# Queries and keys of layer 0 for two pairs at once, 512 columns to a matmul, in a two-layer graph attention kernel

## What is computed

```
q, k, v = x @ Wq + bq, x @ Wk + bk, x @ Wv + bv          # 8 heads of 32
attn = softmax(where(adj == 0, -inf, q k^T / sqrt(32)))
x1 = layernorm(attn v @ Wo + bo + x) * gamma + beta
q, k, v = x1 @ Wq1.T + bq1, ...                          # layer 1
pros = softmax(where(adj == 0, -16384, q k^T))
z = v;  4 times: z = 0.9 * pros z + 0.1 * v
out = layernorm(x1 + z) * gamma1 + beta1
```

## Time and profile before

| | us |
|---|---|
| median of three runs | 782.94 |
| lowest, highest | 782.71, 784.09 |
| span of the profiled execution | 784.0 |
| PE busy in it | 754.1 |
| ACT, DVE, POOL busy | 665.7, 637.1, 547.8 |

### The profile page before, as it was taken

The page is one execution under the profiler, slowest core; times in us unless marked ns, Lnnn a source line. Parts: engine busy times, 40 slices in busy tenths (PEclk is TensorE's granted clock), DMA queues, the critical chain, the costliest instruction groups (busy, mean ns, idle before and its releaser), DMA issues.

```text
span 784.0 us, 32528 instructions
## 1 busy us (share of the span) xinstructions
PE 754.1 (96%) x11544; PEld 710.6 (91%) x11544; DVE 637.1 (81%) x3093; ACT 665.7 (85%) x2570; POOL 547.8 (70%) x417
## 2 busy tenths in 40 slices
PE   6889999999999999999999999999999999999974
PEld 6778999999999999999999999999999999998863
DVE  5778888888888888888888888888888888887765
ACT  4779998889889988988998898998889899899661
POOL 0336858666777777777787777787777778768774
PEclk9899999999999999999999999999999999999997
DMA  7101011010111101111111011111001111100002
GB/s 239 48 21 50 23 35 37 22 30 23 50 50 49 50 29 26 47 50 49 50 49 30 23 51 50 49 49 50 29 23 50 50 50 36 30 16 17 29 15 68
DMA packets 33245, 34.12 MB, mean 44 GB/s; under 512 B 2368, under 2 KB 28864, under 8 KB 33088
## 3 DMA queue, kind: packets, MB, share of 16 engines
q1 hardware_dynamic: 33088, 32.06, 13.8%
HBM read 23.67 MB, written 8.39 MB: 41 GB/s over the span
## 4 chain that ended last, share of the span: by engine, by line
PE 89%; DVE 3%; ACT 2%; issue 2%; DMA 1%; SPq 1%; POOL 1%; POOLq 0%; DVEq 0%; ACTq 0%
PE psF L342 23%; PE psF L411 18%; PE psF L351 16%; PE psF L401 15%; PE psS L391 9%; PE psF L456 7%; PE psF L436 2%; ACT ex L1011 2%; DMA w_raw<-in_w 1%; DVE sm L1400 1%; DMA out<-o_t 1%; SPq L284 0%; DVE o_t L1491 0%; DVE bst L1450 0%; POOL o_t L1927 0%
## 5 line engine op out<-in xcount | busy, mean ns | idle before, releaser
L1011 ACT ACTIVATE ex<-sm,nmax 128x128 f32<-128x128 f32 x1024 | 397.9, 397 | 3.3 <-DVE nmax L1400 2.3
L1859 POOL TENSOR_TENSOR pr<-ex,rec 128x1024 f32<-128x1024 f32 x128 | 245.3, 1918 | 101.1 <-DVE rec L1409 101.1
L1400 DVE CUSTOM_DVE_ANT_0 sm<-psS,mask 128x128 f32<-128x128 f32 x1024 | 228.3, 284 | 41.6 <-PE psS L391 41.4
L1011 ACT ACTIVATION_READ_ACCUMULATOR ex<-sm,nmax 128x1 f32 x1024 | 200.7, 196 | 0.0
L1022 ACT ACTIVATE pT<-psF 128x512 f32<-128x512 f32 x256 | 138.8, 596 | 34.5 <-PE psF L401 34.4
L401 PE MATMUL psF<-ident,pr 128*128 128x128 f32 x1024 | 137.8, 276 | 0.8 <-ACT pT L1022 0.5
L401 PEld LDWEIGHTS psF<-ident,pr 128*128 128x128 f32 x1024 | 112.7, 141 | 9.3 <-ACT pT L1022 0.9
L342 PE MATMUL psF<-xh,w_hi 128*128 128x256 f32 x512 | 112.6, 302 | 7.7 <-DVE w_lo L1339 5.7
L411 PE MATMUL psF<-pT,z 128*32 128x128 f32 x3072 | 103.1, 276 | 2.3 <-DVE z L1512 2.0
L342 PE MATMUL psF<-xh,w_lo 128*128 128x256 f32 x512 | 104.1, 285 | 0.0
L342 PE MATMUL psF<-xl,w_hi 128*128 128x256 f32 x512 | 103.6, 284 | 0.0
(11 more groups left out here) (76 smaller groups left out, 1425.7 us busy)
## 6 DMA issues: line engine op xcount, KB each, us to landing
xt_in<-in_x_t SPq DMA_DIRECT2D x32, 256.0 KB, 3.0
x_in<-in_x SPq DMA_DIRECT2D x32, 256.0 KB, 3.0
out<-o_t SPq DMA_DIRECT2D x30, 256.0 KB, 2.2
adj_in<-in_adj SPq DMA_DIRECT2D x32, 128.0 KB, 2.4
pT<-in_w SPq DMA_DIRECT2D x4, 256.0 KB, 4.0
row<-in_rows SPq DMA_DIRECT2D x1, 768.0 KB, 6.8
w_raw<-in_w SPq DMA_DIRECT2D x3, 256.0 KB, 7.0
out<-o_t SPq DMA_DIRECT2D x4, 128.0 KB, 1.7
```

The costliest lines, as they stand in the source:

```text
L1011: e = nc.scalar.activation(ex[l][:, b, h, :], sm[l][:, b, h, :], ACT.Exp, scale=-1.0, bias=nmax[l][:, b, h:h + 1], accum_out=tot[l][:, b, ...
L1400: last = nc.vector.tensor_tensor_reduce(sm[l][:, b, h, :], psS[:, o:o + N], mask[p.parity][:, b, :], -1.0, BIG, ALU.add, ALU.min, nmax[l][ ...
L1859: nc.gpsimd.tensor_tensor(pr[l][:, b, :, :], ex[l][:, b, :, :], rec[l][:, b, :].unsqueeze(2).broadcast_to([128, H, N]), ALU.mult).then_inc ...
```

## The change

Queries and keys of layer 0 are no longer made for one pair in each turn. An even turn t makes the queries of pairs t and t + 1, an odd turn the keys of pairs t - 1 and t, with 512 moving columns: `two_pairs(c, t)`, six matmuls for one half c of the output features, c = 0 into bank F[0], c = 1 into F[2]. For this xh and xl of layer 0 get two buffers of two pairs each, qT two of two pairs, kT one; x is rounded three pairs further ahead (`split_hi(t + 2)`, `split_lo(t + 3)`), and SP loads `xt_in` three pairs further ahead. Pairs 0 to 5 keep the old way; the first new group, the queries of pairs 6 and 7, stands in `begin()`, and `end()` loses the queries and keys of pair 31.

```diff
@@ SP
             def step(t):
-                load_xt(t + 2)
+                if t.number <= 3:
+                    load_xt(t + 2)
+                elif t.number <= 6:
+                    load_xt(t + (t.number - 2))
+                    load_xt(t + (t.number - 1))
+                else:
+                    load_xt(t + 5)
                 store(t - 9)
@@ PE
+            def two_pairs(c, p):
+                if p.real:
+                    first = p - p.parity
+                    x_ready(0, first + 1)
+                    i = p.number // 2 % 2
+                    for n, (a, e) in enumerate(parts):
+                        for kc in range(C):
+                            last = nc.tensor.matmul(ps_two[c][:, :], (w_hi, w_lo)[e][:, p.parity, kc, c * 128:(c + 1) * 128],
+                                                    (xh0, xl0)[a][i][:, kc, :], start=(n == 0 and kc == 0),
+                                                    stop=(n == 2 and kc == C - 1))
+                    last.then_inc((qr, kr)[c][0].sem, 2)
...
             def scores(l, p):
                 if p.real:
-                    pe.wait_ge(q_s[l].sem, q_s[l].at(p))
-                    pe.wait_ge(k_s[l].sem, k_s[l].at(p))
+                    saved = p + (1 - p.parity) if l == 0 and p.number >= FIRST_TWO else p
+                    pe.wait_ge(q_s[l].sem, q_s[l].at(saved))
+                    pe.wait_ge(k_s[l].sem, k_s[l].at(saved))
@@ PE, begin
                 free((q_s[0], Pair(5)))
+                two_pairs(0, Pair(6))
+                free((q_s[0], Pair(6)))
                 hop(0, Pair(1))
...
                 free((k_s[0], Pair(5)))
+                two_pairs(1, Pair(6))
+                keys(1, 1, Pair(3))
+                free((k_s[0], Pair(6)))
                 turn_hop(0, Pair(1))
-                keys(1, 1, Pair(3))
@@ PE, step
-                queries(0, 0, t - 1)
+                two_pairs(0, t)
                 free((hT_s[3], t - 7))
                 values(1, 0, t - 4)
-                queries(0, 1, t - 1)
                 values(1, 1, t - 4)
...
-                keys(0, 0, t - 1)
-                keys(0, 1, t - 1)
+                two_pairs(1, t)
@@ PE, end
                 values(1, 1, Pair(28))
-                free((z_s[1], Pair(26)))
-                queries(0, 0, Pair(31))
-                queries(0, 1, Pair(31))
                 free((y_s, Pair(29)))
                 turn_probs(1, 1, 0, Pair(27))
                 free((pT_s[1][0][1], Pair(27)))
                 turn_probs(1, 1, 1, Pair(27))
-                free((v_s[1], Pair(28)))
-                keys(0, 0, Pair(31))
-                free((q_s[0], Pair(31)))
+                free((z_s[1], Pair(26)))
                 turn_probs(1, 0, 0, Pair(27))
-                keys(0, 1, Pair(31))
                 free((pT_s[1][1][1], Pair(27)))
                 turn_hop(3, Pair(25))
@@ ACT
             def split_hi(p):
                 if p.real:
                     act.wait_ge(xt_s.sem(p), xt_s.at(p))
-                    act.wait_ge(vr[0].sem, vr[0].at(p - 1))
-                    nc.scalar.activation(xh[0][:, :, :], xt_in[p.parity][:, :, :], ACT.Copy).then_inc(xh_s.sem, 1)
+                    act.wait_ge(vr[0].sem, vr[0].at(p - 4))
+                    nc.scalar.activation(x_of(0, p)[0], xt_in[p.parity][:, :, :], ACT.Copy).then_inc(xh_s.sem, 1)
@@ ACT, begin
                 split_hi(Pair(5))
+                split_hi(Pair(6))
...
                 save_oh(Pair(3))
+                split_hi(Pair(7))
                 save_v(0, Pair(4))
...
                 save_x1h(Pair(3))
+                split_hi(Pair(8))
@@ DVE
+            def save_two(c, p):
+                if p.real:
+                    ready, saved = (qr, kr)[c][0], (q_s, k_s)[c][0]
+                    dve.wait_ge(ready.sem, ready.at(p))
+                    if p.parity == 0:
+                        dve.wait_ge(sr[0].sem, sr[0].at(p - 3))
+                        nc.vector.tensor_scalar(qT0[p.number // 2 % 2][:, c, :], ps_two[c][:, :], SCALE, bq0s[:, c:c + 1],
+                                                ALU.mult, ALU.add).then_inc(saved.sem, 1)
+                    else:
+                        dve.wait_ge(sr[0].sem, sr[0].at(p - 2))
+                        nc.vector.tensor_scalar(kT0[:, c, :], ps_two[c][:, :], col[:, BK0c, c:c + 1], None, ALU.add
+                                                ).then_inc(saved.sem, 1)
@@ DVE, begin
                 split_lo(Pair(5))
+                split_lo(Pair(6))
                 mask_scores(1, 0, 0, Pair(2))
...
                 save_ol(Pair(3))
+                split_lo(Pair(7))
...
                 save_k(0, Pair(5))
+                save_two(0, Pair(6))
...
                 add_hop(0, Pair(1))
+                split_lo(Pair(8))
                 mask_scores(1, 0, 1, Pair(3))
...
-                split_lo(Pair(6))
+                split_lo(Pair(9))
```

More of the change, by code:

```diff
@@ L130, in raw @@
             return w_raw[i - 4][:, :, :]
-        xh = [sb(f"xh{l}", [128, C, T], F32R) for l in range(2)]
-        xl = [sb(f"xl{l}", [128, C, T], F32R) for l in range(2)]
-        qT = [sb(f"qT{l}", [128, C, T]) for l in range(2)]
-        kT = [sb(f"kT{l}", [128, C, T]) for l in range(2)]
+        xh0 = [sb(f"xh0_{i}", [128, C, 2 * T], F32R) for i in range(2)]
+        xl0 = [sb(f"xl0_{i}", [128, C, 2 * T], F32R) for i in range(2)]
+        qT0 = [sb(f"qT0_{i}", [128, C, 2 * T]) for i in range(2)]
+        kT0 = sb("kT0", [128, C, 2 * T])
+        xh1 = sb("xh1", [128, C, T], F32R)
+        xl1 = sb("xl1", [128, C, T], F32R)
+        qT1 = sb("qT1", [128, C, T])
+        kT1 = sb("kT1", [128, C, T])
         sm = [sb(f"sm{l}", [128, 2, H, N]) for l in range(2)]
@@ L255, in run, with half, x_of, q_of @@
                 step(Pair(t))
+        def half(p):
+            return slice(T * p.parity, T * p.parity + T)
+        def x_of(l, p):
+            if l:
+                return xh1[:, :, :], xl1[:, :, :]
+            i = p.number // 2 % 2
+            return xh0[i][:, :, half(p)], xl0[i][:, :, half(p)]
+        def q_of(l, p):
+            return qT0[p.number // 2 % 2][:, :, half(p)] if l == 0 else qT1[:, :, :]
+        def k_of(l, p):
+            return kT0[:, :, half(p)] if l == 0 else kT1[:, :, :]
         def both(r):
@@ L378, in values @@
                     weight(p, 4 * l + 2)
-                    project([lambda kc, m=m: m[:, kc, b * N:(b + 1) * N] for m in (xh[l], xl[l])], b, 4 * l + 2,
+                    project([lambda kc, m=m: m[:, kc, b * N:(b + 1) * N] for m in x_of(l, p)], b, 4 * l + 2,
                             ps_v[l], vr[l])
@@ L390, in scores @@
                                 o = 512 * g + (b * C + c) * N
-                                last = nc.tensor.matmul(psS[:, o:o + N], qT[l][r, c, b * N:(b + 1) * N],
-                                                        kT[l][r, c, b * N:(b + 1) * N], start=True, stop=True)
+                                last = nc.tensor.matmul(psS[:, o:o + N], q[r, c, b * N:(b + 1) * N],
+                                                        k[r, c, b * N:(b + 1) * N], start=True, stop=True)
                     last.then_inc(sr[l].sem, 1)
@@ L1036, in save_x1h @@
                     act.wait_ge(vr[1].sem, vr[1].at(p - 1))
-                    nc.scalar.activation(xh[1][:, :, :], ps_x1[:, :].rearrange("p (c t) -> p c t", c=C), ACT.Copy
+                    nc.scalar.activation(xh1[:, :, :], ps_x1[:, :].rearrange("p (c t) -> p c t", c=C), ACT.Copy
                                          ).then_inc(x1h_s.sem, 1)
@@ L1350, in split_hi @@
                     dve.wait_ge(xt_s.sem(p), xt_s.at(p))
-                    dve.wait_ge(vr[0].sem, vr[0].at(p - 1))
-                    nc.vector.tensor_copy(xh[0][:, :, :], xt_in[p.parity][:, :, :]).then_inc(xh_s.sem, 1)
+                    dve.wait_ge(vr[0].sem, vr[0].at(p - 4))
+                    nc.vector.tensor_copy(x_of(0, p)[0], xt_in[p.parity][:, :, :]).then_inc(xh_s.sem, 1)
             def split_lo(p):
@@ L1373, in save_q @@
                     dve.wait_ge(qr[l].sem, qr[l].at(p))
-                    dve.wait_ge(sr[l].sem, sr[l].at(p - 1))
+                    dve.wait_ge(sr[l].sem, sr[l].at(p - (1 if l else 4)))
                     raw = ps_q[l][:, :].rearrange("p (c t) -> p c t", c=C)
                     if l:
-                        last = nc.vector.tensor_tensor(qT[l][:, :, :], raw, along(b1_col[:, 0, :]), ALU.add)
+                        last = nc.vector.tensor_tensor(q_of(l, p), raw, along(b1_col[:, 0, :]), ALU.add)
                     else:
-                        last = nc.vector.scalar_tensor_tensor(out=qT[l][:, :, :], in0=raw, scalar=SCALE,
+                        last = nc.vector.scalar_tensor_tensor(out=q_of(l, p), in0=raw, scalar=SCALE,
                                                               in1=along(bq0s[:, :]), op0=ALU.mult, op1=ALU.add)
@@ L1701, in step @@
                 make_mask(t - 1)
-                split_lo(t)
+                split_lo(t + 3)
```

40 lines of the change are left out of this document (22 added, 18 removed).

## The result

The changed kernel is slower: 790.97 us median of 6 runs (788.12 to 793.79), against 783.12 (782.52 to 787.33) for the kernel before on the same chip, a ratio of 1.0092 [1.0067, 1.0117]. The ratio is not the quotient of the two medians (that is 1.010), and stands for 7.2 us. The forecast was 782.5 us with a range from 779.7 to 785.4. The profiled run took 788.12 us, the shortest of the six, with a span of 786.0.

A forecast was written before the change was run, and what follows sets the result against it. PE, busy 96% of the span, was taken to bound the kernel. Start-up +6.1, turns -6.0 and end -0.5 made -0.4 us on the 784.0 us span: 783.6, or 782.5 us as median; range 779.7 to 785.4.

The forecast's parts named there:

- The turn: 25 turns of step: twelve 512-column matmuls at 216 ns replace 24 at 118 ns, 0.24 us less each, 6.0 us in all.
- the half-clock row: Two 256-column matmuls start 0.43 us apart at half clock, 213 ns each: one column per 1.2 GHz clock, nothing else.
- a floor of some 109 ns per matmul: In the turn: some 109 ns pass per matmul whatever its width, read from twelve 128-column transposes taking 1.31 us.
- The estimate by the page alone: Turn priced by the skill page's gap, 109.2 and 215.8 ns: 31 ns gained a turn, 0.8 us in all.
- Rival 3: Turns: 512 columns cost what two times 256 cost, so turns give nothing; sum +5.8, 788.8 us; chance 0.09.
- The start-up: Before the turns: two groups pulled ahead (2.60) and waits of 0.94, 0.23, 2.0 and 0.3: 6.1 us later.
- the wait for F[0]: Start-up, after the first new group: PE waits for DVE's save of bank F[0], 0.9 us near 100 us.
- The 2.0 us ahead of the scores: Start-up near 88 us: POOL's product delays split_lo(6) and the masks, so PE stands still 2.0 us.
- lower bound of 4.0: Start-up's least cost, 4.0 us, if DVE gets in ahead of POOL's product and no second meeting follows.
- The rest of pair 8: Start-up, split_lo(8) near 104 us ahead of pair 3's masks: 1.7 us more if met by POOL; counted 0.3.
- The end: end() loses pair 31's four groups, 2.8 us of PE work, but ACT's saves hold it: 0.5 us gained.
- rival 2: Start-up costs more: PE's 2.0 us pause at 88 us lowers its clock; 784.2, or 785.2 us with a further wait; chance 0.18.

The follow-up runs named there:

- e4: Separate test kernel of 60-matmul runs per shape, quiet and beside working engines: 120, 173.5 and 227.5 ns at 256, 384 and 512 columns of rounded fp32.
- e3: Changed kernel with each 512-column matmul cut into two of 256 columns on the same data: 791.31 us, 1.0084 of the kernel before.
- after: The changed kernel as first measured and profiled: median 790.97 us, 1.0092 of the kernel before; profiled run 788.12 us.
- e2: Changed kernel, unedited, run again for a second profile: 792.38 us, 1.0096 of the kernel before.
- e5: Changed kernel plus 24 filler matmuls of 256 columns, results unread, where pair 31's queries and keys stood in the end: 787.08 us, 1.0054.
- e7: Changed kernel with two start-up moves: DVE's split_lo(7) later, layer 1's queries of pair 3 between first two-pair group and hop: 790.50 us, 1.0069.
- e8: Changed kernel with both e5's filler in the end and e7's two start-up moves: 785.46 us, 1.0018 of the kernel before.
- e9: e8 with DVE's split_lo(6) also moved, to behind the two normalisations of pair 3: 786.83 us, 1.0037.
- e10: e8 with the start-up's first two-pair group 256 columns wide instead of 512, pair 7's queries left out: 785.72 us, 1.0028.
- e11: e7 with pair 26's second hop moved into the end's pause, ahead of the turn of pair 25's last hop; no filler: 786.85 us, 1.0040.
- e12: e11 with e9's move of split_lo(6) added, no filler: 786.68 us, 1.0026 of the kernel before.

## Why the prediction was wrong

**The turn: the failed step.** The term was -6.0 us, "I take 216" ns for a 512-column matmul within bounds of 213 and 236. It is 232, and the term is -1.3. The mistake is visible in the prediction's own working. It took 118 ns from the trace for the old matmul, with its 11 ns over the columns, and a price almost without surplus for the new one; the two don't belong to one scale. Two reasons were given. One was the half-clock row, where 213 ns is exactly 256 columns at 1.2 GHz. That row shows only that the surplus is hidden at half clock. It says nothing on full clock, where both kernels run. The other was a floor of some 109 ns per matmul "whatever its width", read from transposes, which 256 columns would only just meet. In e4 384 columns take 160 ns by themselves, far above such a floor, and carry the same 13.5 ns; and the earlier trace rows has 32 score matmuls in 1.10 us, 34 ns each. e4 shows the surplus on every width from 256 to 512 and nearly none in bf16, and e3 shows in this kernel that the width is worth 0.06 us a turn.
The Trainium skill (TensorE: Matmul & The Clock Gate, Back-to-back issue gap) gives N/2.4 + 2.5 ns, for what it calls the isolated gap; for a stream with weight loads it has some 131 ns at 512 columns. e4, such a stream, agrees with the first in bf16 (109 and 216) and with neither for rounded fp32 (120 and 227). The estimate by the page alone, 0.8 us in all, was nearer to the measured 1.3 than the forecast, since it put the same surplus on both sides; its size, 2.5 ns, isn't that of this kernel.

Rival 3 (0.09, 788.8 us) named this mechanism, nearly to its size. It is still 2.2 us short of the measured time, since the share of the clock, below, isn't in it.

**The start-up: right in sum, not always by its parts.** Forecast 6.1, measured 5.6 to 5.8 in after and e2, and 6.7 in e5 (27.8 us). The groups cost 2 x 1.42 instead of 2 x 1.30; the wait for F[0] was 0.8, forecast 0.9. The 2.0 us ahead of the scores stand in about half of the traces; where DVE got in first, the delay came back behind `split_lo(7)` and the mask as 1.2 us ahead of `turn_probs(1, 1, 0)`, which the prediction let "run beside this stall". So its lower bound of 4.0 for "DVE first" was wrong, and that 6.1 is close owes something to luck. The Trainium skill (SBUF — State Buffer, Who interferes with whom) says that the order of issue decides who blocks; e7 and e8 show both orders, 10 to 70 ns apart. The rest of pair 8 took 1.34 us near 107 us and no scores waited.

**The end: right in the trace, wrong in the runs.** PE gained 0.4 us (forecast 0.5), since ACT's saves hold this place. But the pause of 1.9 us left in PE let the clock fall, in three of four traces with the pause (e2, e3, e7; not in after) and in none with it filled or cut up (e5, e8, e9, e10, e11, e12). By the runs, 26 of 30 were low with the pause as it is (after, e2, e3, e7) and 25 of 66 with it filled or cut up. So the pause makes stretches at half clock more likely, not certain. One fall costs 1.6 us (23.1 instead of 21.5 us for the first step of `end()`). The prediction had this mechanism as rival 2, at a pause in the start-up, where the clock stayed at 1.00 even after 1.8 us, and left it out where it took 2.8 us of covered work away.

**The sum.** By the traces the change makes 5.7 - 1.3 - 0.4 = +4.0 us, up to 5.0 with the longer start-up. e5 has the same without the 0.4, 4.4 to 5.4, and measures +4.2 [2.4, 6.0]. The clock adds to this: a median of 0.990 instead of 0.993 over 785 us is 2.4 us, an estimate. Together 6.4 to 7.4, of 7.2 [5.2, 9.2] measured by the ratio (7.9 by the medians). **Open:** e5 and e11 took 3.1 and 2.3 us off (give or take some 2.5 us) where one fall costs 1.6. The traces of after and e7 are of executions 2.9 and 4.6 us shorter than the medians of their runs, at higher clocks than these; where the median run has its further half-clock stretches isn't on record. e2's, near its median, has a second one at 747.1, after the late store; how often a store comes late, and why one pause of PE lowers the clock and another of the same length doesn't, wasn't settled.

## What to carry to other kernels

Price old and new form of an instruction by the same rule: if the measured one exceeds its columns, expect the wider one to do so too, and measure it by itself before building on it. The gain from merging two was 4 ns a pair of matmuls in this kernel (12.5 in the quiet test) and not 20. Work pulled ahead into a stage that PE bounds costs there in full, while the same work taken out of a stage that another engine bounds gives nothing. And covered work may be what keeps the clock up: look at how long the hole is that it leaves, and put other work that is ready into it. Last, one trace is one execution: here two of the same kernel differed by 4 us through a late store and the clock, about as much as the change costs by the traces.

## What was unexpected in the hardware

- In e4 a rounded-fp32 matmul with 128 rows and columns of weights costs its columns at 2.4 GHz plus 13 to 14 ns at 256, 384 and 512 columns (120, 173.5, 227.5 ns); bf16 plus 2.5. Working neighbours change nothing. In this kernel it was 118 and 232 ns at 256 and 512.
- Alone DVE's addition with two SBUF inputs of 512 elements takes 0.69 to 0.70 us. Beside POOL's 30 products of 1024 elements 30 additions took 2.27 us each, one every 2.30 us, as if each waited for a whole product: nine of them in the time of nine. In e4, DVE and POOL in order of time:

```profile
81.34 20.68 DVE L115 TENSOR_TENSOR va<-vb,vc 128x512 f32<-128x512 f32 x9
```

```profile
80.73 20.74 POOL L126 TENSOR_TENSOR pb<-pa 128x1024 f32<-128x1024 f32 x9 [79.05 <-PE bank L71]
```

and, when POOL has finished, one of them in the chain of waits:

```profile
154.72 0.70 DVE va L115
```

- The mask, a TENSOR_SCALAR from int32 to fp32 within SBUF, seems to be blocked in the same way. It took 1.37 us in e2, 0.41 in e7, 1.04 in e8, 0.75 in e12 and 1.38 in e5, and in each of these five it ended 0.14 to 0.16 us after the instruction that POOL was working on. In e2:

```profile
87.74 1.37 DVE L1408 TENSOR_SCALAR mask<-adj_in 128x256 f32<-128x256 int32 x1
```

- Adding 24 matmuls that nobody needs made this kernel 0.4% faster (1.0054 against 1.0092 and 1.0096), and with the calmer start-up 0.5% (1.0018 against 1.0069).
- The same store of 256 KB landed 2.1 to 2.3 us after its issue in ten traces, and 3.5, 3.5 and 4.1 us in after, e12 and e2.
